# A gated cross-attention and feed-forward block on one core: order of the first layer norm, the quantiser half, the gate sums and the head scaling

## The reference

```
_layernorm(x):  (x - m) / jnp.sqrt(v + eps)

# attention, per batch, q = _layernorm(x), k = v = ctx
ig = concat(q, k, v) @ igate_kernel + igate_bias
fg = concat(q, k, v) @ fgate_kernel + fgate_bias
log_fg = jax.nn.log_sigmoid(fg)                      # per head
log_D  = tril(cumsum(log_fg) differences) + ig.T
D = exp(log_D - max_log_D)
C = (q @ k.T / sqrt(64)) * D
normalizer = maximum(abs(C.sum(-1)), exp(-max_log_D))
h = C / (normalizer + 1e-6) @ v
h = h * rsqrt(mean(square(h)) + 1e-6)                # per head
x = x + tanh(g_xattn) * h

# feed-forward: bitlinear(x, w) = act_quant(x) @ weight_quant(w).T
g = bitlinear(x, w_gate); u = bitlinear(x, w_up)     # x = _layernorm(x)
x = x + tanh(g_ffn) * bitlinear(square(relu(g)) * u, w_down)
```

## Time and profile before

| | us |
|---|---|
| median of 3 runs | 664.43 |
| the runs | 663.75, 664.43, 667.57 |
| the profiled execution, its own time | 669.24 |
| its span on the core | 667.5 |
| PE busy, share | 581.0, 87% |
| DVE busy, share | 540.1, 81% |
| ACT busy, share | 453.7, 68% |
| POOL busy, share | 122.1, 18% |

### The profile page before, as it was taken

How to read it: one execution, slowest core, us unless ns; L and a number is a source line. 1 busy time by engine, 2 the same in 40 slices (tenths; PEclk the granted TensorE clock), 3 DMA queues, 4 the chain that set the end, 5 groups by cost and what they waited for, 6 DMA issues and landing times.

```text
span 667.5 us, 18342 instructions
## 1 busy us (share of the span) xinstructions
PE 581.0 (87%) x6517; PEld 342.6 (51%) x6596; DVE 540.1 (81%) x1144; ACT 453.7 (68%) x926; POOL 122.1 (18%) x266
## 2 busy tenths in 40 slices
PE   7583658898999989898999989898999989899896
PEld 4351434655555555555555555555555555646443
DVE  3489567897888979798888979797889989797964
ACT  4465869766684867667684867667685867768562
POOL 1256131112020202012020202112020202112100
PEclk9586779998998999899998999898999999999998
DMA  8884305040130405041130405041140405020000
GB/s 313 300 287 149 129 1 175 2 171 22 55 138 16 174 0 190 0 136 54 64 125 16 174 0 190 0 146 44 41 148 16 174 0 190 1 81 17 17 33 31
DMA packets 45169, 63.73 MB, mean 95 GB/s; under 512 B 1872, under 2 KB 26704, under 8 KB 45136
## 3 DMA queue, kind: packets, MB, share of 16 engines
q1 hardware_dynamic: 45136, 63.30, 27.3%
HBM read 54.77 MB, written 8.52 MB: 95 GB/s over the span
## 4 chain that ended last, share of the span: by engine, by line
PE 61%; DVE 13%; ACT 12%; issue 8%; DMA 5%; DVEq 1%; SPq 1%; POOL 0%; ACTq 0%; POOLq 0%
PE ub L1086 14%; PE gb L1086 14%; PE yb L1112 12%; PE ab L1120 5%; PE tp L1133 5%; PE ab L1100 4%; DMA stage<-in_w_up 2%; ACT hq L544 2%; DVE ssq L884 2%; ACT dmat L570 2%; PE ab L1121 2%; DVE q L823 2%; DMA max_rows<-mrow 1%; ACT dmat L564 1%; DVE ysq L899 1%
## 5 line engine op out<-in xcount | busy, mean ns | idle before, releaser
L524 ACT ACTIVATE relu<-gb 128x512 f32<-128x512 f32 x128 | 75.5, 590 | 101.9 <-PE gb L1086 101.5
L1086 PE MATMUL gb<-wgT,xqT 128*128 128x512 bf16 x479 | 131.8, 394 | 7.0 <-issue 5.3
L1086 PE MATMUL ub<-wuT,xqT 128*128 128x512 bf16 x498 | 135.5, 395 | 2.5 <-DVE stage L756 1.8
L1112 PE MATMUL yb<-wdT,stage 128*128 128x512 bf16 x483 | 115.4, 381 | 4.3 <-issue 2.2
L756 DVE TENSOR_TENSOR stage<-relu,ub 128x512 f32<-128x512 f32 x128 | 87.0, 680 | 19.1 <-ACT relu L526 11.4
L1086 PEld LDWEIGHTS ub<-wuT,xqT 128*128 128x128 bf16 x512 | 52.0, 102 | 65.1 <-issue 9.3
L526 ACT ACTIVATE relu<-relu 128x512 f32<-128x512 f32 x128 | 80.7, 631 | 4.1
L1120 PE MATMUL ab<-qT,cT 64*128 64x256 f32 x256 | 55.2, 446 | 27.7 <-DVE dmat L863 27.7
L1086 PEld LDWEIGHTS gb<-wgT,xqT 128*128 128x128 bf16 x512 | 47.1, 102 | 52.1 <-issue 5.7
L863 DVE SCALAR_TENSOR_TENSOR dmat<-ab,dmat 128x384 f32<-128x384 f32 x128 | 65.4, 551 | 9.4 <-PE ab L1121 6.3
L1112 PEld LDWEIGHTS yb<-wdT,stage 128*128 128x128 bf16 x512 | 47.1, 98 | 50.1 <-issue 3.1
(11 more groups left out here) (110 smaller groups left out, 886.3 us busy)
## 6 DMA issues: line engine op xcount, KB each, us to landing
dmat<-max_rows SPq DMA_DIRECT2D x16, 1024.0 KB, 5.1
values<-in_ctx_v SPq DMA_DIRECT2D x16, 520.0 KB, 7.7
xs<-in_x SPq DMA_DIRECT2D x16, 512.0 KB, 6.0
cT<-in_ctx_t SPq DMA_DIRECT2D x16, 512.0 KB, 6.9
out<-stage SPq DMA_DIRECT2D x32, 256.0 KB, 2.0
stage<-in_w_gate SPq DMA_DIRECT2D x4, 1024.0 KB, 13.6
stage<-in_w_up SPq DMA_DIRECT2D x4, 1024.0 KB, 11.2
stage<-in_w_down SPq DMA_DIRECT2D x4, 1024.0 KB, 5.3
```

Of the source, the lines that this page charges most:

```text
L524: nc.scalar.activation(relu[:, c % 2, :], gb[c % 2][:, :], ACT.Relu).then_inc(g_free, 1)
L1086: last = nc.tensor.matmul(bank[c % 2][:, :], xqT[par][:, t, d, :], w[:, d, c * CH:(c + 1) * CH], start=(d == 0), stop=(d == KD - 1))
L1112: done = nc.tensor.matmul(yb[:, :], hqT[:, c, :], wdT[:, c, :], start=(c == 0), stop=(c == KF - 1))
```

## The change

1. DVE: in `step`, `attention_norm(m)` is called behind `weigh(n, 7)` instead of ahead of `weigh(n, 4)`.
2. ACT: `attention_rstd(m)` is called ahead of `quantise_high(b - 1, 1)` instead of behind it.
3. DVE: `head_squares` is cut in two; the two small products go into `mean_squares(n)`, called behind `gates_in(m)`. `log_forget(m)` is called ahead of `scale_heads(n)` instead of behind it.
4. ACT: `forget_gate(m)` is called ahead of `head_rms(n)` instead of behind it.
5. ACT: a second call of `exp_minus_max(1, 1)` in the prologue is gone; the one in step 0 is left.

No instruction is added; one ACT instruction of 128x16 is removed. The line numbers of the changed kernel are one lower from L631 on in the ACT part and in most of the DVE part, and a few higher behind `head_squares`.

```diff
--- before.py
+++ after.py
@@ -628,7 +628,6 @@
             exp_minus_max(0, 0)
             forget_gate(1)
             magnitudes(0, 2, 1)
-            exp_minus_max(1, 1)
             for p in range(NP):
                 exponentials(0, p, 0)
             magnitudes(1, 0, 2)
@@ -665,12 +664,12 @@
                 if n is not None:
                     heads(n, 0)
                     exponentials(n, 3, npar)
+                if m is not None:
+                    attention_rstd(m)
                 if prev:
                     quantise_high(b - 1, 1)
                 else:
                     magnitudes(2, 2, 6)
-                if m is not None:
-                    attention_rstd(m)
                 relu_square(b, 0, 2)
                 if n is not None:
                     heads(n, 1)
@@ -689,10 +688,10 @@
                     for t in range(T):
                         columns(m, qT[par], t)
                 quantise_high(b, 0)
+                if m is not None:
+                    forget_gate(m)
                 if n is not None:
                     head_rms(n)
-                if m is not None:
-                    forget_gate(m)
                 if third:
                     scale_weight(2, 2)
                     scale_weight(2, 3)
@@ -884,6 +883,8 @@
                     nc.vector.tensor_reduce(ssq[:, t, :], ysq[:, t, :].rearrange("p (h d) -> p h d", d=HD),
                                             axis=AX_X, op=ALU.add).then_inc(post_step, 1)
 
+            def mean_squares(n):
+                k = POST_K * n + 1
                 dve.wait_ge(post_step, k + 5)
                 nc.vector.scalar_tensor_tensor(zz[:, :, :], ssq[:, :, :], 1.0 / HD, rn[:, :, :],
                                                ALU.mult, ALU.mult).then_inc(post_step, 1)
@@ -971,6 +972,7 @@
             magnitudes(1, 3)
             normaliser(0, 0)
             head_squares(0)
+            mean_squares(0)
             weight_scale(1)
             dve.wait_ge(winv_step, WINV[1])
             nc.vector.tensor_tensor(wprod[:, 0:1], wmean[:, 0:1], wmean[:, 0:1], ALU.mult).then_inc(winv_step, 1)
@@ -999,8 +1001,6 @@
                     weigh(n, 2)
                     weigh(n, 3)
                 hidden(b, 0, 1)
-                if m is not None:
-                    attention_norm(m, par)
                 if n is not None:
                     weigh(n, 4)
                     weigh(n, 5)
@@ -1008,6 +1008,8 @@
                 if n is not None:
                     weigh(n, 6)
                     weigh(n, 7)
+                if m is not None:
+                    attention_norm(m, par)
                 hidden_max(b, 0, 0)
                 hidden(b, 0, 3)
                 if prev:
@@ -1027,9 +1029,11 @@
                 if m is not None:
                     gates_in(m)
                 if n is not None:
+                    mean_squares(n)
+                if m is not None:
+                    log_forget(m)
+                if n is not None:
                     scale_heads(n)
-                if m is not None:
-                    log_forget(m)
                 if prev:
                     output(b - 1, 1, npar)
                 if m is not None:
```

More of the change, by code:

```diff
@@ L1029, in step @@
                 if n is not None:
-                    scale_heads(n)
+                    mean_squares(n)
                 if m is not None:
                     log_forget(m)
+                if n is not None:
+                    scale_heads(n)
                 if prev:
```

## The result

| | before | changed kernel |
|---|---|---|
| median, us | 666.0 (663.75 to 668.22, 4 runs) | 638.35 (637.73 to 638.38, 4 runs) |
| profiled execution, its own time | 669.24 | 638.38 |
| its span | 667.5 | 636.7 |
| ratio | | 0.9583, 95% interval 0.9543 to 0.9622 |

The kernel is 4.2% faster. The predicted 643.0 us was 4.6 too high, the range of 634 to 656 holds the result.

What follows compares the result with a forecast made beforehand. Neither PE (87% busy) nor DVE (81%) was taken as saturated; their waits for each other within a step were the loss. 669.24 - 9.8 (half clock) - 13.0 (steps) - 3.5 (step 0) = 642.9, so 643.0 us; range 634 to 656.

Steps and rivals of the forecast that it cites:

- The scores stall: PE's 1.41 us wait for the weigh of head 4 in each step; claimed to go once the norm moves.
- the sum: Row times added along a step's chain: hidden_max stays at 314.69, a step keeps 0.8 to 0.9 us.
- The wait at hidden_cols: DVE's 0.73 us wait for PE's transposes at 317.80; claimed to go, with DVE 0.73 us earlier from there.
- The half clock: TensorE's lower clock behind the scores stall, 1.63 us in six steps; claimed to go with the stall, 9.8 us.
- The two rivals built on a moved half clock: Lower clock moves behind the a_rows stall: once a step, 664.2 us (chance 0.10); twice, 685.4 us, slower (chance 0.03).
- The stall moves from the cumulative sum to a_rows: PE's 0.99 us wait for logf goes; PE instead stands about 1.3 us at a_rows, 13 times.
- The gain of a step: Time kept in each of steps 1 to 13: 1.0 us taken, 13.0 us in all, bounds 0 to 31 us.
- the edge of the overlaps: Step gain of 1.15 us if rows pipeline tighter than added, independent instructions starting before their forerunner's end.
- Step 0, 3.5 us: PE's 3.83 us stall at 79.14 in step 0 goes; 3.5 us gained, bounds 0 and 5.
- Edits 2 and 5 nothing: Swapping rstd and quantiser half on ACT, and the prologue's exp_minus_max, were each claimed to change nothing.
- the step term: The forecast's share from steps 1 to 13: 13 x 1.0 = 13.0 us.

Runs made afterwards that it cites:

- e3_warm: Kernel before plus four dead 512-wide products on PE before the scores of head 6, steps from 1 on; 659.55 us, ratio 0.9892.
- e1_norm: Kernel before with only the norm moved behind weigh 7 and rstd ahead of the quantiser half; 642.4 us, ratio 0.9634.
- e6_enm_kept: Changed kernel with the second exp_minus_max(1, 1) put back in the prologue; 636.98 us, ratio 0.9558 against the kernel before.
- e2_gates: Kernel before with only the gate sums, log_forget and forget_gate moved ahead (edits 3 and 4); 669.46 us, ratio 0.9963.
- e4_cum_early: Changed kernel with cumulative(m), which makes the tile a, called ahead of output(b - 1, 1) on DVE; 628.44 us, ratio 0.9412 against the kernel before.
- e7_rstd_back: Changed kernel with attention_rstd behind the quantiser half again on ACT; 636.31 us, ratio 0.9536 against the kernel before.

## Why the prediction was right, and what was off

- **The scores stall goes, DVE's hidden_max does not move.** Held. The hidden of chunk 2 starts at 332.54, a step earlier at 332.54 - 35.22 = 297.32, and hidden_max at 299.76: 2.44 us, where the sum had 2.45. From a_rows to the next hidden_max it is 314.69 - 290.08 = 24.61 us before and 299.76 - 275.16 = 24.60 after.
- **The wait at hidden_cols goes and DVE runs 0.73 us earlier from there.** Held in kind, short in size, see below.
- **The half clock goes, 9.8 us.** Held: 6 of 6 longer steps vanished, and e3_warm with e1_norm shows that without the idle time of that stall there is none. The prediction's reading that the stretch begins right behind the stall was too narrow: by windows of 0.1 us it begins 1.0 to 1.8 us behind the stall's end, when PE is at the end of the scores or already at the 512-wide products that follow them. It counted the six steps of the profiled execution, without a reason why the stall cost the clock in six and not in twelve, and none was found. The rule of the Trainium skill ("TensorE: Matmul & The Clock Gate", section "A second HAM failure mode: psum-queue depth-cycling") says that short idles between groups of 512-wide products can make the clock swing. In steps 1 to 13 they did not: the stall of 0.92 us at a_rows, and in e1_norm one of 1.24 us at the cumulative sum, left the clock at 1.00. Longer ones outside these steps did stand beside a lower clock: 2.39 us in front of 512-wide products in step 0 of the changed kernel (until 102.12, lower from about 101.5), and 2.22 us in its last step (until 626.89, lower from 627.1), while the same 2.22 us in e6_enm_kept had no lower clock behind them. So it is not shown whether the scores stall brought the lower clock by its place among small products or by being longer (1.41 against 1.24). The two rivals built on a moved half clock fell.
- **The stall moves from the cumulative sum to a_rows.** Held: 0.92 us in each of 13 steps, against about 1.3 expected. The cumulative sum itself was expected 2.3 us earlier and came 2.39 earlier (8.31 us behind hidden_max instead of 10.70); a_rows stands less than expected because a came earlier, see the next point. e2_gates shows this move by itself (0.99 turns into 0.89, worth 0.20), and e4_cum_early that a_rows is what the step hangs on.
- **The gain of a step: the mis-sized term.** I took 1.0 us for each of 13 steps, 13.0 us; it was 1.40, 18.2 us. The sum had given 0.8 to 0.9 and named 1.15 as the edge of the overlaps. It was made with bracketed idle times and lengths of rows, and both hide the overlap of neighbours. From hidden_max to hidden_cols there were 3.11 us before and 2.26 after, so the wait at hidden_cols was worth 0.85 and not its 0.73. From hidden_cols to the gate sums I had 317.07 to 321.87, 4.80 us, and it took 4.55: the normaliser no longer waited for ACT (0.1: it starts 0.59 us behind hidden_max's last reduce, before 0.70), and the gate sums started before the reduce had ended, as they do not need it. From scl to a I had 2.4 us; it was 2.22. These are 0.12 + 0.25 + 0.18 = 0.55 us of the same kind, which with the 0.83 of the sum make 1.4.
- **Step 0, 3.5 us.** Prologue and step 0 together gave 3.7. That this is so close is partly luck, as the part varies by about 1 us between executions: PE's 3.83 us in front of the scores are gone, as the sum said, but how they and the other waits of step 0 add up to 3.7 was not worked out.
- **Edits 2 and 5 nothing.** Held (e7_rstd_back, e6_enm_kept).

So of the 4.6 us by which the forecast was off, the step term accounts for 13 x 0.4 = 5.2 us, the prologue and step 0 for 0.2, and the one longer step for 0.7 the other way.

## What to carry to other kernels

When an engine waits in front of an instruction that nobody needs soon, put behind it what others wait for; but follow the chain to the next meeting point, for the stall turns up at the first thing that is still queued behind the same work (here the tile a behind the head scaling and the output, worth another 15 us once it was moved). Add up distances between starts from one meeting point to the next, and not lengths and bracketed waits; and since TensorE can be granted a lower clock behind a stall (here behind one of 1.41 us in six steps of twelve, 1.63 us each), compare the lengths of equal steps and their granted clocks.

## What the runs showed that I had not expected

- Four dead 512-wide products in a 1.41 us stall made the kernel before 1.1% faster (0.9892, 0.9841 to 0.9944) and its 4 runs lie within 3 us, where the 13 of the kernel before beside them spread over 7 (more runs also spread more).
- The two residual adds, one on DVE and one on POOL, slow each other, and the one that starts first keeps its speed. Before, POOL started ahead of DVE by a third of a microsecond; after, DVE by 0.01 us. Timeline of the kernel before:

```profile
326.00 1.26 POOL L436 TENSOR_TENSOR x<-ysq,xs 128x512 f32<-128x512 f32 x1 [5.39 <-DVE stage L806]
...
326.33 1.48 DVE L907 TENSOR_TENSOR x<-ysq,xs 128x512 f32<-128x512 f32 x1
```

And of the changed kernel:

```profile
310.24 0.68 DVE L908 TENSOR_TENSOR x<-ysq,xs 128x512 f32<-128x512 f32 x1
...
310.25 1.81 POOL L436 TENSOR_TENSOR x<-ysq,xs 128x512 f32<-128x512 f32 x1 [5.54 <-DVE stage L805]
```

DVE's add fell from 1.48 to 0.68 us and POOL's rose from 1.26 to 1.81. e1_norm, where the order of output and csum is still bound to PE, has 1.48 and 1.26 again; e2_gates has 0.68 and 1.80. DVE's busy time of a step fell by 1.0 us, 0.8 of it in this add. It did not enter the step's length: both adds stand behind a, and from a_rows to the next hidden_max it is 24.6 us either way. This is what the Trainium skill ("SBUF — State Buffer", section "SBUF: two separate sides") says of the ports that the two engines share: they are an exclusive lock, also for a DVE instruction with two inputs in SBUF, and the one that starts first has it. The rows agree in who is slowed, by 0.8 us on DVE or 0.5 us on POOL; that it is these ports no run here shows.
